# GpSimd's state sums and gating one slot later, and the gated y loaded in two halves

## The reference, cut to what matters

```python
h = layernorm(x) * (1 + ca) + sa
# Mamba block, for every token t and channel d, over 16 states n
val, gate = split(h @ W_in); val = silu(conv(val)); B, C = val @ W_B, val @ W_C
Delta = softplus((val @ W_delta + delta_base) @ W_tau)
dA = -Delta * exp(A_log)
state[n] = exp(dA) * state[n] + expm1(dA) / (dA + 1e-6) * Delta * B[n] * val      # a scan over the tokens
y = sum_n state[n] * C[n]
x = x + ga * (y * silu(gate) @ W_out + h)
# mixture of 8 experts (the best two of each token) and one shared expert
h = layernorm(x) * (1 + cb) + sb
x = x + gb * (sum_e gate_e * (gelu(h @ W1_e + b1_e) @ W2_e + b2_e) + shared(h))
```

## Time and profile before

| | us |
|---|---|
| median of 3 runs | 4778.74 (4776.73 to 4779.63) |
| profiled execution | 4777.7 |
| its span | 4775.9 |
| TensorE busy (PE) | 3858.5 |
| VectorE busy (DVE) | 4037.8 |
| ScalarE busy (ACT) | 3984.7 |
| GpSimd busy (POOL) | 3649.5 |
| granted clock of TensorE, mean | 0.887 |

### The profile page before, as it was taken

The page is one execution under the profiler, slowest core; times in us unless marked ns, Lnnn a source line. Parts: engine busy times, 40 slices in busy tenths (PEclk is TensorE's granted clock), DMA queues, the critical chain, the costliest instruction groups (busy, mean ns, idle before and its releaser), DMA issues.

```text
span 4775.9 us, 37136 instructions
## 1 busy us (share of the span) xinstructions
PE 3858.5 (81%) x9708; PEld 1637.4 (34%) x9708; DVE 4037.8 (85%) x3892; ACT 3984.7 (83%) x4397; POOL 3649.5 (76%) x2308
## 2 busy tenths in 40 slices
PE   6633514888889898898888998898889887989889
PEld 3211101334333333333343333333333433333344
DVE  1388799999999999999999999999999998788730
ACT  2788898998989897998989897989989897978811
POOL 0499887787878888888879897888888787767621
PEclk8856756999999999999999999999999997989889
DMA  4678857888887888788888888888887886667541
GB/s 136 229 219 264 254 140 218 224 236 248 228 249 216 258 225 259 212 249 243 234 248 230 251 227 243 236 252 225 242 253 225 232 226 163 182 168 195 149 135 66
DMA packets 352221, 1037.19 MB, mean 217 GB/s; under 512 B 41253, under 2 KB 44389, under 8 KB 344710
## 3 DMA queue, kind: packets, MB, share of 16 engines
q1 hardware_dynamic: 278282, 766.35, 47.0%
q0 software_dynamic: 73728, 268.47, 28.6%
HBM read 639.74 MB, written 126.51 MB: 160 GB/s over the span
## 4 chain that ended last, share of the span: by engine, by line
PE 22%; issue 16%; ACT 15%; POOL 15%; DVE 12%; DMA 10%; SPq 0%; POOLq 0%; DVEq 0%; ACTq 0%
DMA ysum<-hs 9%; PE ps L1113 7%; PE ps L1132 6%; POOL inv L1374 5%; PE ps L1083 3%; POOL hs L1347 3%; ACT inv L760 3%; DVE ps L1179 3%; DVE ps L1173 3%; DVE ps L1167 3%; POOL ysum L1361 2%; ACT inv L753 2%; DVE hs L1197 2%; ACT abar L775 2%; ACT th L771 1%
## 5 line engine op out<-in xcount | busy, mean ns | idle before, releaser
L1374 POOL TENSOR_TENSOR inv<-inv,th 128x1024 f32<-128x1024 f32 x512 | 1257.7, 2456 | 164.6 <-ACT th L771 162.6
L1113 PE MATMUL ps<-hf,w1r 128*128 128x512 f32 x2304 | 1120.3, 639 | 92.1 <-DMA w1r<-in_W 55.3
L1347 POOL TENSOR_TENSOR hs<-hs,Cb 128x1024 f32<-128x1024 f32 x384 | 966.3, 2516 | 43.2 <-DVE hs L1197 26.6
L1132 PE MATMUL ps<-w2r,hid 128*128 128x512 f32 x1776 | 824.9, 612 | 1.9 <-ACT xn L873 1.9
L1150 PE MATMUL ps<-Brow,pick 48*128 48x512 bf16 x1024 | 338.2, 413 | 592.7 <-DVE hs L1197 592.3
L1167 DVE SCALAR_TENSOR_TENSOR ps<-ps,us 128x1024 f32<-128x1024 f32 x512 | 628.2, 1227 | 200.2 <-PE ps L1150 199.8
L771 ACT ACTIVATE th<-delta,halfA 128x1024 f32<-128x1024 f32 (+1 forms) x640 | 607.8, 969 | 190.6 <-POOL inv L1374 190.4
L753 ACT ACTIVATE inv<-nrd,kappa 128x1024 f32<-128x1024 f32 (+1 forms) x640 | 578.3, 972 | 154.1 <-DVE ps L1179 154.1
L1361 POOL DMA_DIRECT2D ysum<-hs x480 | 431.8, 900 | 349.2 <-DMA ysum<-hs 339.9
L1179 DVE SCALAR_TENSOR_TENSOR ps<-ps,inv 128x1024 f32<-128x1024 f32 x512 | 627.8, 1226 | 73.2 <-POOL inv L1374 51.4
L1186 DVE SCALAR_TENSOR_TENSOR ps<-nrd,inv_kappa,ps 128x1024 f32<-128x1024 f32 (+1 forms) x640 | 675.1, 1073 | 15.6
(11 more groups left out here) (155 smaller groups left out, 5059.5 us busy)
## 6 DMA issues: line engine op xcount, KB each, us to landing
ysum<-hs POOLq DMA_DIRECT2D x512, 512.0 KB, 5.6
Cb<-c_rows SPq DMA_DIRECT2D x384, 512.0 KB, 4.5
w1r<-in_W SPq DMA_DIRECT2D x144, 512.0 KB, 5.7
w2r<-w_scaled SPq DMA_DIRECT2D x141, 512.0 KB, 7.0
Cb<-c_rows SPq DMA_DIRECT2D x128, 256.0 KB, 3.7
gbc<-expert_gates SPq DMA_DIRECT2D x128, 256.0 KB, 5.2
aw<-in_W_val SPq DMA_DIRECT2D x64, 256.0 KB, 6.4
xa<-in_x SPq DMA_DIRECT2D x32, 512.0 KB, 6.7
```

Of the source, the lines that this page charges most:

```text
L1113: mm = t.matmul(o, w1r[:, n % 2, k, h * P:(h + 1) * P], hf[:, k, :], start=(k == 0), stop=(k == G - 1))
L1132: mm = t.matmul(o, hidden(e)[:, h, tt * P:(tt + 1) * P], (last_w2(e) if q == NQ - 1 and grp == 1 else w2r[:, e % 3])[:, h, :], start=(grp ...
L1347: gp_.tensor_tensor(hs[:, c % 4, :], hs[:, c % 4, :], Cb[:, c % 2, :], ALU.mult).then_inc(hC_done, 1)
L1374: gp_.tensor_tensor(inv[:, c % 6, :], inv[:, c % 6, :], th[:, c % 2, :], ALU.mult).then_inc(thinv_done, 1)
```

## The change

GpSimd's `add_to_y` and `gate_y` stand where they stood within a slot, but `add_to_y` handles state c-2 in place of c-1, and `gate_y` runs at r = 2 and 18. SyncE stores the gated y at r = 3 and 19. The load of `gyin` is two DMAs of 512 KB in steps 3 and 4, for groups 0 and 1 and for groups 2 and 3; the first waits only for the units that hold its groups, the second for all. TensorE's first out job waits for 32 counts per block in place of 16.

```diff
--- before.py
+++ after.py
@@ -578,10 +578,12 @@
                 tt = r - 2
                 sp.wait_ge(ev_w2, 12 * qp + 8 + tt + 1)
                 sp.dma_start(out_flat[qp * T + tt * P:qp * T + (tt + 1) * P, :], x1[:, tt, :]).then_inc(out_st[tt], 16)
-            if r == 3 and has(qf):
-                sp.wait_ge(gy_st, 16 * units_before_end(qf))
+            if r in (3, 4) and has(qf):
+                lo = 2 * (r - 3)
+                size = [n for q, n in BLOCKS if q <= qf < q + n][0]
+                sp.wait_ge(gy_st, 16 * (units_before_end(qf) - (0 if lo else size)))
                 ge(sp, f_gates, qf)
-                sp.dma_start(gyin, gy_d[qf // 2, :, :, columns(qf)].rearrange("g p t -> p g t")).then_inc(gy_ld, 16)
+                sp.dma_start(gyin[:, lo:lo + 2, :], gy_d[qf // 2, lo:lo + 2, :, columns(qf)].rearrange("g p t -> p g t")).then_inc(gy_ld, 16)
             if r in (3, 4, 5, 6) and has(qf):
                 tt = r - 3
                 ge(sp, out_st[tt], 16 * qf)
@@ -694,7 +696,7 @@
                     sp.wait_ge(B_ready, N * FIRST_U[k - 1])
                 lo = BROW * (k % 2)
                 sp.dma_start(Brow[lo:lo + 3 * N, 0:n * T], row.rearrange("j n t -> (j n) t")).then_inc(B_ld[k % 2], 16)
-            if r in (2, 18) and 0 <= c // N - 1 < NU:
+            if r in (3, 19) and 0 <= c // N - 1 < NU:
                 u = c // N - 1
                 sp.wait_ge(y_gated, u + 1)
                 sp.dma_start(rows_of(gy_d, u), tile_of(gy[:], u)).then_inc(gy_st, 16)
@@ -1075,7 +1077,7 @@
                     mm.then_inc(mm_bc, 1)
                 elif kind == "out":
                     if i == 0:
-                        pe.wait_ge(gy_ld, 16 * (q + 1))
+                        pe.wait_ge(gy_ld, 32 * (q + 1))
                         pe.wait_ge(wo_ld, 16 * (q + 1))
                         pe.wait_ge(h_ld, 16 * (q + 1))
                         pe.wait_ge(f_dga, q // QPB + 1)
@@ -1395,9 +1397,9 @@
             for H, step in steps_of(c):
                 pool_steps(pool, H, step)
             weight(c + 2)
-            if r in (1, 17):
+            if r in (2, 18):
                 gate_y(c // N - 1)
-            add_to_y(c - 1)
+            add_to_y(c - 2)
 
             f = c + 6
             if 0 <= f < 2 * NF * NB:
```

## The result

The changed kernel takes 4907.36 us (median; 4907.04 to 4916.01), the kernel before 4777.73 in the same session: ratio 1.0284, 95% interval 1.0271 to 1.0297. It is 130 us slower by the medians, 136 by the ratio. The forecast was 4890, slower, with a range of 4820 to 4930.

A forecast was written before the change was run, and what follows sets the result against it. VectorE, 94% busy in the twelve windows, was taken as the bound. Terms 87 + 10 + 6 + 26 + 0 = 129 us, less 17 given back, put +112 on 4777.7: 4890 us, range 4820 to 4930.

The forecast's parts named there:

- Part 1, the late second half: Second half, behind tile 2's store in SyncE's queue, delays TensorE's out job: 7.9 us a window, 87 over eleven windows.
- The stall: TensorE before the out job, waiting for the second half to land: mean 6.6 us a window in blocks 1 to 11.
- The clock's part: TensorE's matmuls run slower after standing idle: 1.6 us a window, bounds 0 and 3.0.
- the missing slack at B of slot 8: VectorE already waits for TensorE's product B there, so it is late by all of TensorE's delay less 0.3 us.
- VectorE's waits for B: Sign: behind the out job's stall, VectorE's waits for TensorE's product B grow by about 90 us.
- Blocks 12 to 15: Late load in the last blocks: 10 us for block 12, 6 for 13 to 15 together, including the tail.
- Part 2, the scan's wait for a sum: VectorE's scan needs a sum that lands later: 2.2 us a window, 26 us over twelve windows.
- there is no such wait in VectorE's next slots: Step: at slots 30 to 0 no later VectorE wait absorbs the scan's delay, so 2.2 us a window stay lost.
- waits at 27 that vanish in return: Sign the forecast is wrong: VectorE's existing waits at slot 27 disappear in exchange for the new ones.
- Part 3, the moved gating: GpSimd's gating moves to slots 2 and 18, making 18 heavy; VectorE does not wait there: 0, bounds -5 and +5.
- GpSimd's waits for sums: Sign: GpSimd's total wait for sums to land stays near 340 us, since the sums' spacing is unchanged.
- The give-back of 17 us: VectorE's old waits, 10 us a window, shrink where their makers are less held up: 1.4 a window.

The follow-up runs named there:

- halves_only: Kernel before with only the gated y's load changed: two halves, the second in step 4 behind the store of output tile 2; 4882.14 us, ratio 1.0231.
- both_in_3: Changed kernel with both halves loaded in step 3, except block 12, which keeps its second half in step 4; 4831.18 us, 1.0128 of the kernel before.
- half_in_5: halves_only with the second half in step 5, behind the store of output tile 3; 4997.75 us, 1.0468 of the kernel before.
- late_12: Kernel before with block 12's load of the gated y alone moved to step 4, behind the store of output tile 2; 4784.77 us, ratio 1.0025.
- hs3: Kernel before with three scan buffers in place of four, so scan c waits for the sum of state c-3; nothing moved; 4772.41 us, ratio 0.9999.
- hs3_heavy: hs3 with gating one column wide in slots 1 and 17 and idle same-size GpSimd multiplications in 2 and 18; 4792.96 us, 1.004 of the kernel before.
- hs3_halves: hs3 and halves_only together, sums and gating in their old slots; 4874.19 us, 1.021 of the kernel before.
- half_first: Changed kernel with step 4's second half issued ahead of the store of output tile 2; 4853.51 us, 1.0172 of the kernel before.

## Why the prediction was right, and where it was not

**Part 1, the late second half: right in mechanism, and nearly in size.** Forecast 87 us for blocks 1 to 11; halves_only lost 89 in these windows, and in the changed kernel the late half is worth some 75, its distance to both_in_3. The stall was forecast at 6.6 us; it was 5.1 to 7.8 in the changed kernel, 70.7 in all or 6.4 a window. Two errors in it cancel in part: the half was issued 1.4 us after TensorE was free, not 1.1, and landed in 4.9 us on average, not 5.4. The clock's part was taken as 1.6: the four out jobs, from the start of the first matmul of L1083 to the end of its last and without the product B between them, took 16.8 to 19.6 us before (mean 17.9), and 18.9 on average after, 1.0 more. That TensorE's lateness is passed on in full was argued from the missing slack at B of slot 8; half_in_5 shows it, 113 us for 111 of idle. One sign was named wrongly: VectorE's waits for B did not grow by 90 us but fell to 58.0, because it now waits ahead of them, in the eviction of the first out job (51.3 us).

The Trainium skill's fit for a DMA that GpSimd issues ("DMA: Bandwidth & Descriptors", "Anatomy of one DMA") would have had the half land in 3.2 us. The second halves, which SyncE issues, took 3.8 to 7.3 us, those of blocks 1 to 12 4.8 on average.

**Blocks 12 to 15: 16 forecast, 20 measured** between the scans of slots 448 and 480, none after, none in the tail. late_12 shows 12 of it, for block 12.

**Part 2, the scan's wait for a sum: the waits came, the price was wrong.** The prediction read the places well (0, 13, 25, 26, 30), and expected the ones at 13, 25 and 26 free; it held those at 30 to 0 for lost, 2.2 us a window. hs3 has all of these waits and costs nothing. The failed step is "there is no such wait in VectorE's next slots": there was one at slot 1, 1.87 us on average and mostly for ScalarE's `uu`, and one at slot 10, 1.88 us and mostly for TensorE before `hT`; in hs3 they are 0.14 and 0.43. The earlier trace rows shows only the two longest waits, 123 of 158 us, and the prediction took them for all ("10 us a window"). Its sign of being wrong, waits at 27 that vanish in return, came true (from 5.4 to 1.2 us a window), but it speaks of the scans' waits at 25 and 26, not of the late half.

**Part 3, the moved gating: priced at 0, costs some 20 (12 to 26 by hs3_heavy's interval).** The failed step is "both weights made there are used several us later": true, but the weight is not the only thing that GpSimd makes there. The sum stands behind the gating, and with the scan's shorter reach it is what VectorE waits for at slot 21. The shorter reach alone is free, as hs3 shows. Whether the moved gating alone, with four buffers' reach, would be free too, no run shows; their combination was not weighed. That GpSimd's waits for sums would stay near 340 us was wrong too: in the changed kernel they are 252.1 us.

**The give-back of 17 us** was a guess between bounds, with no place named. The runs show one of that size. halves_only is 110 over and both_in_3 61, and block 12's late half, 12, is in both; without counting it twice that is 159, and the changed kernel is 136 over, 23 less. Of these, 8 us are TensorE's: before the out jobs of blocks 1 to 11 it idled 79.0 us in halves_only and 70.7 in the changed kernel, where the second halves landed in 4.9 us on average and not in 5.7. Why they landed sooner, and where the other 15 us are saved, is not shown.

So the forecast was 103 for the load (87 and 16), 26 for the shift and 17 back, 112 in all; the runs have 110, 49 (both_in_3 without block 12) and 23 back, 136 in all. The mis-sized term is the shift. That the terms without the give-back add up to 129, which is the difference of the two spans, is luck.

**Still open.** both_in_3 is 61 over before. The moved gating (19) and block 12 (12) are 31 of it, its own 5.7 us of TensorE idle in blocks 1 to 11 perhaps 7. Its profiled execution, at 4824.24 us, is 51 over 4773. Between 13 and 23 us have no experiment of their own. A candidate is the longer wait at slot 21: against hs3's trace VectorE idles 20 us more there in both_in_3 and 12 more in hs3_heavy, where no sum stands a slot later. That hs3_halves comes out 8 us below halves_only goes, for 6.5 us, with less idle time of TensorE, since its second halves land in 5.1 us on average in blocks 1 to 11 and not in 5.7; why they do is open. Two kernels that would settle more were not tried: the moved gating with the sums in their old slots and four buffers, and the changed kernel with five scan buffers, which would take the scan's wait away directly.

## What to carry to other kernels

Before a load is moved one step on in a queue, read what will stand ahead of it there and what that waits for: the second half was late less by its slot than by a store that waited for VectorE (with the half ahead of that store, in half_first, 54 of the 81 us of idle time went). In hs3 a wait that appeared on the bounding engine was taken off the next ones in full; so compare the sum of all its waits, not the new one, and not with the longest old ones alone. And where a step moves behind another on an in-order engine, follow every product of that engine, its DMAs too, to its reader.

## What the runs showed that was not expected

Taking away a fourth of the scan buffers of an engine that is 94% busy cost nothing (0.9999), although it then waited 144 us for landings in the whole run. The profile names the wait of a matmul for a load "issue", in all 14 places where TensorE idled before the out job in halves_only; only SyncE's rows tell what it was.
